# First stage's gates: own key dropped from the backward scan, sums of batch 0 by identity products on TensorE, caps behind the exponentials, new orders

## The chip, the cores and the metric

One of the cores of a Trainium2 chip runs the whole program. The metric is device time of one launch in microseconds (us). TensorE (PE) multiplies matrices out of SBUF into PSUM, VectorE (DVE), ScalarE (ACT) and GpSimd (POOL) work elementwise, SyncE (SP) issues most transfers. Each engine runs its own list of instructions in order and waits for the others through semaphores.

## The reference

It is a two-layer model on x (4 batches, 512 positions, 512 channels): a bidirectional decay gate, attention, a second gate, and a mixture of experts. The change touches the first gate alone, of which this is computed for every batch and channel, with k = v = the side input and r = x:

```
ek  = exp(min(k, 30));   ekv = ek * k;   euk = exp(min(u + k, 30))
nf, df = forward scans  a = a * decay + ekv,  b = b * decay + ek
nb, db = the same scans backward
num = nf + nb - ekv + euk * k
den = df + db - ek  + euk
c   = sigmoid(x) * num / max(den, 1e-8) * (0.8 + 0.2 * tf)
```

The value c goes, as a high and a low half (fp32r), into the query, key and value products of the attention.

## The kernel before

Channels lie on the partitions, positions along the free dimension: a gate is one chunk of 128 channels by 512 positions of one batch. `first_gates` (lines 91 to 379) is the first stage: it makes the eight gates n = 0 to 7 of batches 0 and 1 (four chunks each, `KC` = 4) and the 16 query products of batch 0. The stage is one block: `attention` (from line 672) begins when all five engines have ended their lists, with projections of the key rows, a gate of its own kind (lines 1452 to 1505) and the same weight stream. After it come routing and the experts.

The order of the work is written out by hand, one list for each engine (lines 65 to 83). A letter is a step and the number its gate or its query head. On TensorE `k` and `x` are four f32 transposes each (lines 233 and 241) into `psk` (two banks) and `psx` (three banks), `v` the vectors, and `Q` a query product (`split_products`, line 668: twelve fp32r matmuls of 512 columns) into `psq` (two banks). On ScalarE `t` takes the keys out of PSUM (271), `E` is the pair of exponentials (276, 277), `h` the high half of a query weight (265), `F` the sigmoid's denominator 1 + exp(-x) (283 to 291), `c` the high half of c (295), `e` takes a query product out (301). On VectorE `m` is the pair of minima (328, 329), `s` the four scans (344, 345), `f` the fraction (352, 355, 357), `l` the low half of c (334). On GpSimd `o` is ekv (202), `p` the own-key terms euk - ek and (euk - ek) * k (206, 208), `a` the four sums (213 to 218), `q` the low half of a query weight (193). On SP `w` loads a query weight into a ring of four, `O` stores a query product, `X` stores x transposed, `K` and `n` load what the attention needs first (lines 136 to 173).

Each gate's tensors have two halves, used in turn (`n % 2`), so gate n waits for parts of gate n - 2. A query product waits for its weight's low half and for all four low halves of c of batch 0:

```python
pe.wait_ge(u_lo, j + 1)
pe.wait_ge(lo_done, KC)
if j >= 2:
    pe.wait_ge(q_left, j - 1)
```

`dec`, the decays that the scans read, lies in PSUM; in the attention stage the decays lie in SBUF. Elsewhere in the program line 2170 adds a transposed f32 tile onto an open PSUM bank with four f32 products by the identity for each of 16 row tiles, and lines 1061 to 1063 are the fp32r products of the attention's scores, 128 to 512 columns wide.

## Time and profile before

| what | value |
|---|---|
| median of 3 runs | 2301.48 us (2299.45 to 2307.04) |
| the profiled execution | 2301.87 us, span 2300.2 us |
| TensorE busy | 2137.5 us (93%), 11247 matmul records |
| VectorE, ScalarE, GpSimd busy | 1366.6, 1160.0, 1439.5 us |
| granted clock, mean | 0.975 |

Slices of the span, in tenths of busy time (each slice is 57.5 us, so the first stage is the first two):

```profile
PE   2899999999999999999788989999999999999996
DVE  7868888778856676766854633333333333333386
ACT  4477777777767777667562123333333333333310
POOL 7887877788745656666661402456667777753355
```

TensorE is at nine tenths or more in most slices and has its lowest share, two tenths, in the first. The chain that ended last has 32% of the span on TensorE, most of it in the experts, and none of its listed lines lies in the first stage.

### The profile page before, as it was taken

Reading aid. Unit: us, or ns where it says so; the run is one execution under the profiler, and the core shown is the slowest. Engines: PE = TensorE matmul, PEld = TensorE weight load, DVE = VectorE, ACT = ScalarE, POOL = GpSimd, SP = SyncE. Lnnn points to the kernel's source line nnn. Section 1 sums busy time; section 2 is a strip of 40 time slices with the busy share of each in tenths; the row PEclk is TensorE's granted clock in tenths of the full one; section 3 lists DMA queues with packets and bytes.
Section 4 is the critical chain, followed back from the end, with each engine's and each line's share of the span. In section 5 each row is a group of like instructions: output and inputs, shape, how many; then the busy total and the mean of one; then the engine's idle time right before and its main releaser. Section 6 shows DMA issues by size and latency. Waiting matters only on the chain. (4 is left out here: it accounts for less than half of the span.)

```text
span 2300.2 us, 39953 instructions
## 1 busy us (share of the span) xinstructions
PE 2137.5 (93%) x11247; PEld 1860.9 (81%) x11247; DVE 1366.6 (59%) x2499; ACT 1160.0 (50%) x2491; POOL 1439.5 (63%) x961
## 2 busy tenths in 40 slices
PE   2899999999999999999788989999999999999996
PEld 1678888888878878777677869988999999998875
DVE  7868888778856676766854633333333333333386
ACT  4477777777767777667562123333333333333310
POOL 7887877788745656666661402456667777753355
PEclk9999999999999999999897999999999999999998
DMA  5444444543365546665345544556667666664666
GB/s 129 142 124 130 129 133 160 170 126 97 123 216 169 161 119 206 215 203 173 91 134 220 193 153 135 159 156 194 182 188 213 193 209 186 197 197 127 179 196 207
DMA packets 368185, 381.34 MB, mean 166 GB/s; under 512 B 51572, under 2 KB 283576, under 8 KB 363256
## 3 DMA queue, kind: packets, MB, share of 16 engines
q1 hardware_dynamic: 256136, 253.25, 35.9%
q10 hardware_dynamic: 96496, 75.28, 10.7%
q0 software_dynamic: 15360, 50.34, 6.7%
q8 instruction: 109, 1.79, 0.3%
q14 instruction: 84, 0.69, 0.1%
HBM read 265.26 MB, written 121.63 MB: 168 GB/s over the span
## 5 line engine op out<-in xcount | busy, mean ns | idle before, releaser
L2061 POOL TENSOR_SCALAR we_high<-we_raw 128x1408 fp32r<-128x1408 f32 (+1 forms) x94 | 132.3, 1408 | 306.1 <-PE up_e L668 230.4
L2063 POOL TENSOR_TENSOR we_low<-we_raw,we_high 128x1408 fp32r<-128x1408 f32 (+1 forms) x94 | 312.3, 3322 | 7.8
L2276 DVE TENSOR_TENSOR hidden_e<-silu_e,up_e 128x352 f32<-128x352 f32 x127 | 66.2, 521 | 248.3 <-ACT silu_e L2215 248.3
L2259 DVE TENSOR_TENSOR hT_low<-hT_ps,hT_high 128x256 fp32r<-128x256 f32 x127 | 53.9, 425 | 254.4 <-ACT hT_high L2201 254.4
L2215 ACT ACTIVATE silu_e<-gate_e 128x352 f32<-128x352 f32 x127 | 59.1, 466 | 282.0 <-PE up_e L668 270.9
L668 PE MATMUL gate_e<-we_high,xT_high 128*128 x508 | 176.2, 347 | 15.6 <-DVE xT_low L2266 10.4
L2220 ACT ACTIVATE rows_out<-down_e 128x512 f32<-128x512 f32 x127 | 76.0, 599 | 199.4 <-PE down_e L668 199.4
L668 PE MATMUL gate_e<-we_high,xT_low 128*128 x508 | 164.6, 324 | 0.0
L668 PE MATMUL gate_e<-we_low,xT_high 128*128 x508 | 164.1, 323 | 0.0
L668 PE MATMUL up_e<-we_high,xT_high 128*128 x508 | 164.0, 323 | 0.0
L668 PE MATMUL up_e<-we_high,xT_low 128*128 x508 | 163.7, 322 | 0.0
L668 PE MATMUL up_e<-we_low,xT_high 128*128 x508 | 163.1, 321 | 0.0
L668 PE MATMUL down_e<-we_high,hT_high 128*128 x381 | 150.0, 394 | 2.6 <-issue 2.6
L668 PE MATMUL down_e<-we_low,hT_high 128*128 x381 | 150.9, 396 | 0.0
L668 PE MATMUL down_e<-we_high,hT_low 128*128 x381 | 150.8, 396 | 0.0
L1438 DVE TENSOR_TENSOR pT_low<-weights_T,pT_high 128x512 fp32r<-128x512 f32 (+1 forms) x192 | 108.1, 591 | 66.4 <-ACT pT_high L1256 65.1
L942 POOL TENSOR_TENSOR q_low<-q_raw,q_high 128x512 fp32r<-128x512 f32 x64 | 104.1, 1629 | 69.0 <-ACT q_high L1222 68.9
L1239 ACT ACTIVATE prob<-scores,neg_max 128x128 f32<-128x128 f32 (+3 forms) x256 | 131.6, 530 | 17.9 <-DVE neg_max L1423 17.7
L1423 DVE CUSTOM_DVE_ANT_0 scores<-scores,mask 128x128 f32<-128x128 f32 (+3 forms) x256 | 118.0, 522 | 36.5 <-PE scores L1063 36.4
L1248 ACT ACTIVATE prob<-prob,row_inv 128x128 f32<-128x128 f32 (+3 forms) x256 | 122.8, 557 | 26.0 <-DVE row_inv L1431 26.0
L938 POOL TENSOR_TENSOR wV_low<-w_ring,wV_high 128x512 fp32r<-128x512 f32 x64 | 87.6, 1376 | 66.0 <-ACT wV_high L1204 66.0
L938 POOL TENSOR_TENSOR wO_low<-w_ring,wO_high 128x512 fp32r<-128x512 f32 x64 | 95.8, 1504 | 43.2 <-ACT wO_high L1204 43.1
(389 smaller groups left out, 7180.5 us busy)
## 6 DMA issues: line engine op xcount, KB each, us to landing
slots_out<-rows_out ACTq DMA_DIRECT2D x127, 256.0 KB, 2.5
rows_early<-slots_in ACTq DMA_DIRECT2D x500, 64.0 KB, 3.4
we_raw<-L_ffn_w_gate SPq DMA_DIRECT2D x32, 704.0 KB, 4.9
we_raw<-L_ffn_w_up SPq DMA_DIRECT2D x32, 704.0 KB, 5.2
w_ring<-L_attn_Wq SPq DMA_DIRECT2D x64, 256.0 KB, 3.3
q_T<-q_out SPq DMA_DIRECT2D x64, 256.0 KB, 2.5
w_ring<-L_attn_Wk SPq DMA_DIRECT2D x64, 256.0 KB, 3.7
w_ring<-L_attn_Wv SPq DMA_DIRECT2D x64, 256.0 KB, 3.7
```

Source lines behind the costliest of these rows:

```text
L668: last = nc.tensor.matmul(out, a, b, start=start and i == 0, stop=stop and i == len(terms) - 1)
L938: tt(w_split(*u, 1), ring[:, i % RING, :], w_split(*u, 0).bitcast(F32), ALU.subtract).then_inc(u_lo, 1)
L942: tt(head(ql, n), head_raw(n), head(qh, n).bitcast(F32), ALU.subtract).then_inc(q_lo, 1)
L1239: last = nc.scalar.activation(prob[:, n % 2, P_AT[i]:P_AT[i] + w], pss[x_][:, at:at + w], ACT.Exp, scale=-1.0, bias=nmax[:, n % 2, i:i + 1 ...
L1248: nc.scalar.activation(w, w, ACT.Copy, scale=rinv[:, n % 2, i:i + 1]).then_inc(s_norm, 1)
L1423: last = nc.vector.tensor_tensor_reduce(out=acc, in0=acc, in1=mask[:, S - w:], scale=-1.0, scalar=HUGE, op0=ALU.add, op1=ALU.min, accum_ou ...
L1438: tt(ptl[:, at:at + w], pst[(3 * n + x_) % 2][:, 0:w], pth[:, at:at + w].bitcast(F32), ALU.subtract).then_inc(t_lo, 1)
L2061: nc.gpsimd.tensor_scalar(wh[:, p, at:to], raw[:, at:to], 1.0, 1.0, ALU.mult, ALU.mult).then_inc(w_hi, 1)
L2063: nc.gpsimd.tensor_tensor(wl[:, p, at:to], raw[:, at:to], wh[:, p, at:to].bitcast(F32), ALU.subtract).then_inc(w_split, 1)
L2215: nc.scalar.activation(sg[:], psg[:], ACT.Silu).then_inc(s_done, 1)
L2220: nc.scalar.activation(yb[:, p, :], psy[p][:], ACT.Copy).then_inc(y_ev, 1)
L2276: nc.vector.tensor_tensor(hb[:], sg[:], psu[:], ALU.mult).then_inc(h_done, 1)
```

## The change

- **Caps.** ScalarE takes the exponentials straight from the key's PSUM bank, uncapped, with u as the bias of the second one. GpSimd then caps both at exp(30) (and at 3.0e38). The minima of VectorE and the step `E` are gone.
- **Backward scan.** It writes b[t] = (b[t+1] + src[t+1]) * decay over 511 columns, the last column being zero: the backward sum without the own key. The own-key terms then are euk and euk * k alone, one product on GpSimd in place of a difference and a product.
- **Sums.** For gates 0 to 3 TensorE adds eu, df, db into `psq[1]` and dk, nf, nb into `psq[0]` by products with the identity (step `a` in its list); the fraction reads both banks, and the factor and the reciprocal lie in `x_stage` (SBUF) in place of `psx`. For gates 4 to 7 GpSimd adds as before, four sums.
- **Orders.** All five lists are new. `l3` moves behind `s4`, `x5` and `k7` among the query products, and the loads `w`, `K`, `n` ahead of stores.

The diff, cut to its core:

```diff
@@ -38,6 +38,8 @@
 NEG, HUGE = -2.0 ** 100, 3.0e38
 CONSTS = 8
+EXP_30 = float(np.exp(np.float32(30.0)))
+
 V_BQ, V_BK, V_BV, V_W1, V_W2, V_U1, V_U2, V_BO, V_N = 0, 16, 32, 48, 52, 56, 60, 64, 68
@@ -63,24 +65,21 @@
 FIRST_PE = (
-    "k0 v0 k1 x0 k2 x1 k3 k4 x2 k5 k6 x3 x4 k7 x5 Q0 Q1 Q2 Q3 Q4 x6 Q5 Q6 Q7 Q8 Q9 Q10 x7 Q11 Q12 Q13 Q14 Q15 "
+    "k0 v0 k1 x0 k2 x1 a0 k3 x2 a1 k4 a2 x3 k5 a3 x4 k6 Q0 Q1 Q2 x5 Q3 Q4 k7 Q5 Q6 x6 Q7 Q8 Q9 Q10 x7 Q11 Q12 Q13 Q14 Q15 "
 ).split()
 FIRST_ACT = (
-    "t0 t1 E0 E1 h0 F0 t2 h1 E2 h2 h3 t3 c0 F1 h4 E3 t4 h5 c1 h6 F2 h7 F3 E4 F4 t5 h8 E5 c2 h9 c3 e0 t6 h10 e1 t7 "
-    "h11 E6 e2 F5 e3 e4 F6 e5 c4 E7 e6 e7 h12 e8 h13 e9 c5 h14 e10 e11 h15 F7 e12 c6 e13 e14 c7 e15 "
+    "t0 t1 h0 F0 h1 t2 F1 h2 h3 c0 t3 F2 h4 h5 h6 c1 t4 h7 h8 F3 h9 c2 t5 h10 h11 h12 c3 F4 e0 t6 h13 h14 e1 h15 e2 c4 "
+    "F5 e3 e4 t7 c5 e5 e6 F6 e7 e8 e9 c6 e10 F7 e11 e12 e13 c7 e14 e15 "
 ).split()
 FIRST_DVE = (
-    "m0 m1 s0 s1 m2 f0 m3 l0 s2 f1 m4 l1 s3 f2 m5 f3 l2 l3 s4 m6 s5 f4 m7 s6 f5 l4 s7 f6 l5 f7 l6 l7 "
+    "s0 s1 f0 s2 l0 f1 s3 l1 f2 l2 f3 s4 l3 s5 f4 l4 s6 f5 l5 s7 f6 l6 f7 l7 "
 ).split()
 FIRST_POOL = (
-    "o0 p0 o1 p1 a0 a1 o2 q0 p2 q1 q2 o3 q3 a2 p3 q4 q5 a3 o4 q6 p4 q7 q8 o5 q9 p5 q10 a4 q11 o6 a5 p6 o7 p7 q12 "
-    "q13 a6 q14 a7 q15 "
+    "o0 p0 o1 p1 q0 q1 o2 p2 q2 q3 q4 o3 p3 q5 q6 q7 o4 p4 q8 q9 q10 o5 p5 q11 a4 q12 o6 p6 q13 a5 q14 q15 o7 p7 a6 a7 "
 ).split()
 FIRST_SP = (
-    "w4 w5 w6 w7 w8 w9 w10 O0 w11 O1 O2 w12 O3 X4 X5 w13 O4 w14 O5 O6 O7 O8 w15 O9 X6 O10 O11 K0 n0 O12 X7 n1 O13 "
-    "n2 O14 O15 n3 "
+    "w4 w5 w6 w7 w8 w9 w10 w11 w12 w13 w14 w15 O0 X4 O1 O2 O3 X5 O4 O5 O6 O7 K0 n0 O8 n1 O9 X6 O10 n2 O11 n3 O12 X7 O13 O14 O15 "
 ).split()
-
 def turns(order, **steps):
@@ -186,7 +185,7 @@
             pool.wait_ge(ident_steps, 2)
             nc.gpsimd.memset(zero[:], 0.0).then_inc(ident_steps, 1)
             pool.wait_ge(ident_steps, 3)
-            tt = nc.gpsimd.tensor_tensor
+            tt, ts = nc.gpsimd.tensor_tensor, nc.gpsimd.tensor_scalar
             def low(j):
                 pool.wait_ge(u_hi, j + 1)
@@ -196,28 +195,31 @@
             def first_product(n):
                 p = n % 2
                 pool.wait_ge(exp_done, n + 1)
+                ts(ek[:, p, :], ek[:, p, :], EXP_30, HUGE, ALU.min, ALU.min).then_inc(min_done, 1)
+                ts(eu[:, p, :], eu[:, p, :], EXP_30, HUGE, ALU.min, ALU.min).then_inc(min_done, 1)
                 if n >= 2:
                     pool.wait_ge(scan_done, n - 1)
-                    pool.wait_ge(sums_done, 2 * (n - 1))
+                pool.wait_ge(min_done, 2 * n + 1)
                 tt(ekv[:, p, :], ek[:, p, :], kt[:, p, :], ALU.mult).then_inc(products_done, 1)
-            def other_products(n):
+            def other_product(n):
                 p = n % 2
-                tt(dl[:, p, :], eu[:, p, :], ek[:, p, :], ALU.subtract).then_inc(products_done, 1)
-                pool.wait_ge(products_done, 3 * n + 2)
-                tt(dk[:, p, :], dl[:, p, :], kt[:, p, :], ALU.mult).then_inc(products_done, 1)
+                if 2 <= n < KC + 2:
+                    pool.wait_ge(added, n - 1)
+                pool.wait_ge(min_done, 2 * n + 2)
+                tt(dk[:, p, :], eu[:, p, :], kt[:, p, :], ALU.mult).then_inc(products_done, 1)
             def sums(n):
                 p = n % 2
                 pool.wait_ge(scan_done, n + 1)
-                tt(nb[:, p, :], nf[:, p, :], nb[:, p, :], ALU.add)
-                tt(db[:, p, :], df[:, p, :], db[:, p, :], ALU.add).then_inc(sums_done, 1)
-                pool.wait_ge(sums_done, 2 * n + 1)
-                pool.wait_ge(products_done, 3 * n + 3)
-                tt(nf[:, p, :], nb[:, p, :], dk[:, p, :], ALU.add)
-                tt(df[:, p, :], db[:, p, :], dl[:, p, :], ALU.add).then_inc(sums_done, 1)
-
-            turns(FIRST_POOL, o=first_product, p=other_products, q=low, a=sums)
+                tt(df[:, p, :], df[:, p, :], db[:, p, :], ALU.add)
+                tt(nf[:, p, :], nf[:, p, :], nb[:, p, :], ALU.add).then_inc(sums_done, 1)
+                pool.wait_ge(sums_done, 2 * (n - KC) + 1)
+                pool.wait_ge(products_done, 2 * n + 2)
+                tt(df[:, p, :], df[:, p, :], eu[:, p, :], ALU.add)
+                tt(nf[:, p, :], nf[:, p, :], dk[:, p, :], ALU.add).then_inc(sums_done, 1)
+
+            turns(FIRST_POOL, o=first_product, p=other_product, q=low, a=sums)
         @block.tensor
         def _(pe):
@@ -228,7 +230,7 @@
                 if n >= KC:
                     pe.wait_ge(k_in[0], 16 + 16 * KC)
                 if n >= 2:
-                    pe.wait_ge(kt_done, n - 1)
+                    pe.wait_ge(exp_done, n - 1)
                 for t in range(TC):
                     last = nc.tensor.transpose(psk[n % 2][:, t * P:(t + 1) * P], kin[:, n, t, :], ident[:])
                 last.then_inc(k_T, 1)
@@ -249,11 +251,22 @@
                 split_products(nc, psq[j % 2][:], [((qwh[:, j, k, :], qwl[:, j, k, :]), (ch[:, 0, k, :], cl[:, 0, k, :]))
                                                    for k in range(KC)], True, True).then_inc(q_mm, 1)
+            def add(n):
+                p = n % 2
+                pe.wait_ge(scan_done, n + 1)
+                pe.wait_ge(products_done, 2 * n + 2)
+                if n:
+                    pe.wait_ge(c_steps, 3 * n)
+                for ps_, parts in ((psq[1], (eu, df, db)), (psq[0], (dk, nf, nb))):
+                    for i, part in enumerate(parts):
+                        last = nc.tensor.matmul(ps_[:], ident[:], part[:, p, :], start=i == 0, stop=i == 2)
+                last.then_inc(added, 1)
+
             def vectors(n):
                 pe.wait_ge(v_in, 16 * (len(vec) + 1))
                 nc.tensor.transpose(psv, rows[:], ident[0:V_N, 0:V_N]).then_inc(x_T, 1)
-            turns(FIRST_PE, k=keys, v=vectors, x=rows_x, Q=queries)
+            turns(FIRST_PE, k=keys, v=vectors, x=rows_x, a=add, Q=queries)
         @block.scalar
         def _(act):
@@ -265,16 +278,18 @@
                 nc.scalar.activation(qwh[:, j, :, :].rearrange("p k m -> p (k m)"), qraw[:, j % QR, :], ACT.Copy).then_inc(u_hi, 1)
             def keys(n):
+                p, i = n % 2, n % KC
                 act.wait_ge(k_T, n + 1)
                 if n >= 2:
-                    act.wait_ge(products_done, 3 * (n - 1))
-                nc.scalar.activation(kt[:, n % 2, :], psk[n % 2][:], ACT.Copy).then_inc(kt_done, 1)
-
-            def exponentials(n):
-                p = n % 2
-                act.wait_ge(min_done, n + 1)
-                nc.scalar.activation(ek[:, p, :], ek[:, p, :], ACT.Exp)
-                nc.scalar.activation(eu[:, p, :], eu[:, p, :], ACT.Exp).then_inc(exp_done, 1)
+                    act.wait_ge(products_done, 2 * (n - 1))
+                    act.wait_ge(scan_done, n - 1)
+                    if n < KC + 2:
+                        act.wait_ge(added, n - 1)
+                    else:
+                        act.wait_ge(sums_done, 2 * (n - KC - 1))
+                nc.scalar.activation(ek[:, p, :], psk[p][:], ACT.Exp)
+                nc.scalar.activation(kt[:, p, :], psk[p][:], ACT.Copy)
+                nc.scalar.activation(eu[:, p, :], psk[p][:], ACT.Exp, bias=cols[:, V_U1 + i:V_U1 + i + 1]).then_inc(exp_done, 1)
             def factor(n):
                 i, px = n % KC, psx[n % XR]
@@ -284,11 +299,15 @@
                 else:
                     if n >= KC + 2:
                         act.wait_ge(xt_out, 16 * (n - KC - 1))
+                    else:
+                        act.wait_ge(c_steps, 3 * (n - 1))
                     nc.scalar.activation(xst[:, n % 2, :], px[:], ACT.Identity,
                                          bias=cols[:, V_BO + i:V_BO + i + 1]).then_inc(x_left, 1)
                 nc.scalar.activation(px[:], px[:], ACT.Exp, scale=-1.0).then_inc(factor_steps, 1)
                 act.wait_ge(factor_steps, 2 * n + 1)
-                nc.scalar.activation(px[:], px[:], ACT.Identity, bias=one[:]).then_inc(factor_steps, 1)
+                if 2 <= n < KC:
+                    act.wait_ge(c_steps, 3 * (n - 1))
+                nc.scalar.activation(xst[:, n % 2, :] if n < KC else px[:], px[:], ACT.Identity, bias=one[:]).then_inc(factor_steps, 1)
             def c_high(n):
                 act.wait_ge(c_steps, 3 * n + 3)
@@ -310,24 +329,16 @@
             turns(order[:1], t=keys)
             act.wait_ge(t_chain, 1)
             nc.scalar.activation(small[:, 20:24], small[:, 16:20], ACT.Exp, scale=-1.0).then_inc(s_chain, 1)
-            turns(order[1:], t=keys, E=exponentials, h=high, F=factor, c=c_high, e=queries)
+            turns(order[1:], t=keys, h=high, F=factor, c=c_high, e=queries)
         @block.vector
         def _(dve):
             nc.vector.memset(one[:], 1.0)
+            for last_of in (nb, db):
+                nc.vector.memset(last_of[:, :, S - 1:S], 0.0)
             dve.wait_ge(v_in, 16 * (len(vec) + 1))
             nc.vector.tensor_reduce(small[:, 16:20], te[:], AX.X, ALU.add).then_inc(t_chain, 1)
             dve.wait_ge(cols_done, 1)
-
-            def minima(n):
-                p, i = n % 2, n % KC
-                dve.wait_ge(kt_done, n + 1)
-                if n >= 2:
-                    dve.wait_ge(products_done, 3 * (n - 1))
-                    dve.wait_ge(scan_done, n - 1)
-                nc.vector.tensor_scalar(ek[:, p, :], kt[:, p, :], 30.0, None, ALU.min)
-                nc.vector.tensor_scalar(eu[:, p, :], kt[:, p, :], cols[:, V_U1 + i:V_U1 + i + 1], 30.0, ALU.add,
-                                        ALU.min).then_inc(min_done, 1)
             def low(n):
                 dve.wait_ge(hi_done, n + 1)
@@ -336,28 +347,36 @@
             def scans(n):
                 p = n % 2
-                dve.wait_ge(products_done, 3 * n + 1)
+                dve.wait_ge(products_done, 2 * n + 1)
                 if n >= 2:
                     dve.wait_ge(c_steps, 3 * (n - 1))
+                    if n < KC + 2:
+                        dve.wait_ge(added, n - 1)
                 col = dec[:, n:n + 1].broadcast_to([P, S])
-                for f, b, src in ((nf, nb, ekv), (df, db, ek)):
+                after = dec[:, n:n + 1].broadcast_to([P, S - 1])
+                for f, b, src in ((df, db, ek), (nf, nb, ekv)):
                     nc.vector.tensor_tensor_scan(f[:, p, :], col, src[:, p, :], 0.0, ALU.mult, ALU.add)
-                    last = nc.vector.tensor_tensor_scan(b[:, p, ::-1], col, src[:, p, ::-1], 0.0, ALU.mult, ALU.add)
+                    last = nc.vector.tensor_tensor_scan(b[:, p, 0:S - 1][:, ::-1], src[:, p, 1:S][:, ::-1], after, 0.0,
+                                                        ALU.add, ALU.mult)
                 last.then_inc(scan_done, 1)
             def fraction(n):
                 p, px = n % 2, psx[n % XR]
-                dve.wait_ge(sums_done, 2 * n + 2)
+                if n < KC:
+                    dve.wait_ge(added, n + 1)
+                    num, den, fac = psq[0][:], psq[1][:], xst[:, p, :]
+                else:
+                    dve.wait_ge(sums_done, 2 * (n - KC) + 2)
+                    num, den, fac = nf[:, p, :], df[:, p, :], px[:]
                 dve.wait_ge(factor_steps, 2 * n + 2)
-                nc.vector.scalar_tensor_tensor(out=df[:, p, :], in0=df[:, p, :], scalar=1e-8, in1=px[:],
+                nc.vector.scalar_tensor_tensor(out=df[:, p, :], in0=den, scalar=1e-8, in1=fac,
                                                op0=ALU.max, op1=ALU.mult).then_inc(c_steps, 1)
                 dve.wait_ge(c_steps, 3 * n + 1)
-                nc.vector.reciprocal(px[:], df[:, p, :]).then_inc(c_steps, 1)
+                nc.vector.reciprocal(fac, df[:, p, :]).then_inc(c_steps, 1)
                 dve.wait_ge(c_steps, 3 * n + 2)
-                nc.vector.scalar_tensor_tensor(out=px[:], in0=nf[:, p, :], scalar=par1[:, n // KC, n % KC, 2:3], in1=px[:],
+                nc.vector.scalar_tensor_tensor(out=px[:], in0=num, scalar=par1[:, n // KC, n % KC, 2:3], in1=fac,
                                                op0=ALU.mult, op1=ALU.mult).then_inc(c_steps, 1)
-            minima(0)
             dve.wait_ge(s_chain, 3)
             nc.vector.tensor_scalar(small[:, 24:28], small[:, 20:24], 1.0, None, ALU.add).then_inc(t_chain, 1)
             dve.wait_ge(t_chain, 2)
```

## Rows read from the trace of the kernel before

**Rows 1.** Windows of 20 us: length, busy time (instructions) of PE, PEld, DVE, ACT, POOL, clock, DMA.

```profile
20.00:40.00 20.00, 3.23 (x13) 2.52 (x14) 19.90 (x19) 8.02 (x15) 19.69 (x17) 1.00 0.23 63
...
80.00:100.00 20.00, 20.00 (x91) 16.28 (x90) 18.86 (x17) 10.07 (x18) 19.69 (x16) 1.00 0.55 168
```

**Rows 2.** Timeline of VectorE, 16 to 64: start, duration, instruction, idle before.

```profile
16.31 1.21 DVE L344 TENSOR_TENSOR_SCAN g_nf<-vec_ps,g_ekv 128x512 f32<-128x512 f32 x1
...
25.24 0.39 DVE L328 TENSOR_SCALAR g_ek<-g_kt 128x512 f32<-128x512 f32 x1
...
26.96 0.67 DVE L352 SCALAR_TENSOR_TENSOR g_df<-g_df,psx 128x512 f32<-128x512 f32 x1
...
31.73 0.52 DVE L328 TENSOR_SCALAR g_ek<-g_kt 128x512 f32<-128x512 f32 x1
...
62.73 1.45 DVE L334 TENSOR_TENSOR c_low<-psx,c_high 128x512 fp32r<-128x512 f32 x2
```

**Rows 3.** Timeline of all engines at the first stage's end and the attention's start.

```profile
109.84 0.39 PE L668 MATMUL psq<-c_high,wq_low 128*128 128x512 f32 x1
...
111.07 0.68 ACT L301 ACTIVATE q_out<-psq,bqs 128x512 f32<-128x512 f32 x1
112.18 0.50 SPq L160 DMA_DIRECT2D w_ring<-L_attn_Wv  x1
...
113.19 0.42 PEld L1114 LDWEIGHTS proj<-ident,k_rows 128*128 128x128 f32 x4 [3.38 <-issue]
...
116.08 0.63 ACT L1204 ACTIVATE wV_high<-w_ring 128x512 fp32r<-128x512 f32 x1 [0.72 <-DMA w_ring<-L_attn_Wv]
```

**Rows 4.** Timeline of TensorE: first query product, and a start behind a gap in attention.

```profile
64.33 0.77 PE L668 MATMUL psq<-c_high,wq_high 128*128 128x512 f32 x1
64.89 0.63 PE L668 MATMUL psq<-c_low,wq_high 128*128 128x512 f32 x1
65.32 0.63 PE L668 MATMUL psq<-c_high,wq_low 128*128 128x512 f32 x1
...
66.48 0.39 PE L668 MATMUL psq<-c_high,wq_low 128*128 128x512 f32 x1
...
962.17 1.09 PE L1114 MATMUL proj<-ident,k_rows 128*128 128x128 f32 x4 [5.01 <-DVE v_low L1401]
...
963.17 0.41 PE L1062 MATMUL scores<-k_low,q_high 128*128 128x128 f32 x1
963.38 0.41 PE L1063 MATMUL scores<-k_high,q_low 128*128 128x128 f32 x1
```

**Rows 5.** GpSimd: a timeline row, then groups by form (busy us, mean ns | idle).

```profile
13.43 1.26 POOL L202 TENSOR_TENSOR g_ekv<-g_ek,g_kt 128x512 f32<-128x512 f32 x1 [11.28 <-ACT g_eu L277]
...
L2061 POOL TENSOR_SCALAR we_high<-we_raw 128x1408 fp32r<-128x1408 f32 x62 | 85.1, 1372 | 230.4 <-PE up_e L668 230.4
...
L2085 POOL TENSOR_SCALAR we_high<-we_raw 64x512 fp32r<-64x512 f32 x1 | 0.6, 615 | 0.0
```

**Rows 6.** VectorE's groups by form: dearest scan, and a reciprocal in SBUF.

```profile
L1458 DVE TENSOR_TENSOR_SCAN g_db<-par,g_ek 128x512 f32<-128x512 f32 x24 | 49.0, 2040 | 0.0
...
L1500 DVE RECIPROCAL g_db<-g_df 128x256 f32<-128x256 f32 x16 | 27.9, 1743 | 0.0
```

**Rows 7.** f32 on TensorE: loads of four transposes, then line 2170 between others.

```profile
14.52 0.87 PEld L241 LDWEIGHTS psx<-ident,xin 128*128 128x128 f32 x4
...
2201.18 1.05 PE L2170 MATMUL xT_ps<-ident,xT 128*128 128x128 f32 x8
2201.99 0.48 PE L668 MATMUL xT_ps<-we_high,expert_rows_more 128*128 128x512 f32 x1
```

**Rows 8.** Windows around two starts behind gaps, columns as in rows 1.

```profile
114.00:120.00 6.00, 4.77 (x11) 3.80 (x12) 2.30 (x3) 3.34 (x7) 5.92 (x12) 0.51 0.90 272
...
962.00:967.00 5.00, 4.83 (x17) 4.48 (x18) 3.52 (x11) 3.65 (x5) 0.00 (x0) 0.50 0.79 281
```

**Rows 9.** Timeline of ScalarE: the first keys leave PSUM.

```profile
10.59 0.58 ACT L271 ACTIVATE g_kt<-psk 128x512 f32<-128x512 f32 x1
```

4 lines of the change are left out of this document (2 added, 2 removed).

## The prediction

> **What bounds the kernel now.** I read the page's table of slices first: the diff touches only lines 66 to 379, and the stretch that these lines fill is the first 113 us of 2300. Then the windows of 20 us: in the four from 20 to 100 (the first and the last stand in the rows) VectorE is busy 18 to 20 of 20 us and GpSimd 19.7, while TensorE has 3 us of work at 20:40 and is full at 80:100 [rows 1]. So it has two halves. In the first, gates of batch 0 are made by VectorE and GpSimd and TensorE waits; in the second, TensorE makes 16 query products without a gap. The hinge is the fourth low half of c (line 334, `l3`): `Q0` waits for `lo_done >= 4`. It ends at 62.73 + 1.45 = 64.18 [rows 2], the first product starts at 64.33 and the last matmul starts at 109.84 [rows 3]; the attention stage starts at 113.19 [rows 3]. What comes behind follows from there with nothing that is tied to absolute time, so the kernel's change is the shift of 113.19 and little else. From 64.33 on, the products are back to back: 192 matmuls, from the sixth (66.48) to the last (109.84) 0.228 us each if the two groups of transposes among them take 0.43 [rows 3, 4], so relief of GpSimd or VectorE behind that point is worth nothing; what counts is when `l3` comes.
>
> **Prices.** Eight scans go from 16.31 to 25.24, 1.116 us each [rows 2]; a gate has four (4.46). A fraction (lines 352, 355, 357) goes from 26.96 to 31.73, 4.77 us [rows 2]. A pair of minima takes 25.24 to 26.96, 1.72 [rows 2]. A GpSimd tensor_tensor takes 1.26 [rows 5].
>
> **Parts that take work away.** The minima leave VectorE: five pairs stand before `l3` (m1 to m5), some 8.6 us. The reciprocal writes to SBUF instead of PSUM: from SBUF to SBUF 256 columns take 1.74 [rows 6], so 512 3.5, next to the same within the 4.77, no change. The backward scan has one column less and its two operations exchanged; bounds 1.1 (as now) to 2.0 (the dearest scan row of the trace [rows 6]); I take 1.116, as the decay operand stays in PSUM as in the rows of this stage. At the upper end the ten backward scans before `l3` would cost 9 us; I keep that for the range's upper part. On GpSimd a gate of batch 0 falls from 7 tensor_tensor to 2 plus two caps. A cap is a tensor_scalar: 64 partitions by 512 takes 0.615, 128 by 1408 takes 1.37 [rows 5]; 0.5 to 0.75, taken 0.6. GpSimd then has idle time in the whole first half, so its errors cost nothing. ScalarE gets three reads of each key bank in place of one plus two from SBUF: the same count.
>
> **The part that adds: the sums on TensorE.** For gates 0 to 3 six products with the identity, 512 columns of f32, stand between scans and fraction; call their time A. They begin after `scan_done` and, as both PSUM banks are single, after the fraction before (`c_steps >= 3n`). The fraction waits for `added`. So fraction and sums of batch 0 run in one chain, (A + 4.8) per gate, where before GpSimd's four sums (some 5.1 us) ran beside VectorE's work for another gate.
>
> The only f32 product by the identity in the trace is line 2170. Its 4 calls are 8 records, from 2201.18 to 2201.99 [rows 7], so two records a call, 0.10 us a record of 128 columns at the full clock. The f32 transposes at half clock take 0.87 for four, 0.21 each [rows 7]. Neither tells the price of 512 columns: at half clock an fp32r matmul of 128 columns takes 0.21 too [rows 4], while 512 columns take 0.43, so at 128 columns something other than the columns sets the pace. Lower end: twelve records at the fp32r pace, 12 x 0.228 = 2.7 us at 2.4 GHz and 12 x 0.43 = 5.1 at 1.2. Upper end: the record scaled by its columns, 12 x 4 x 0.21 = 10.2 at 1.2 GHz and half of that, 5.1, at 2.4 (by the 0.10, 4.9). I take the upper price: both operands are f32, a call needs two loads of the identity, and if the moving operand is handled in parts like the stationary one each load must meet both parts. The Trainium skill, FP8 and Floating Point Precision, section TensorE Precision Notes, says true FP32 is four passes; by it A would be 5.1 to 10.2, by the lower pace 2.7 to 5.1, and no row here decides.
>
> The clock: behind the last product TensorE has a gap with four transposes at 113.19 in it [rows 3], and the granted clock of 114:120 is 0.51, which is 1.2 GHz [rows 8]. At 962 the same: 0.50 for 5 us of matmuls [rows 8] behind a gap of 5.01 [rows 4]. At 64.33 the slow pace lasted until near 66.48 [rows 4]. Between two sums lie 4.8 us of fraction, with one or two groups of transposes: a gap like these. So each A starts or soon falls to 1.2 GHz and stays there for t = 2.1 to 5.3 us or more: A = 5.1 + t/2, 6.2 to 7.8 (8.5 at t = 6.8). Taken 7.5. The Trainium skill (TensorE: Matmul & The Clock Gate, section What's actually happening) puts it as a throttled default that activity releases. It speaks against placing short bursts on an idle TensorE, and the rows of 114:120 agree.
>
> **The walk to `l3`.** Keys 0 leave PSUM from 10.59 [rows 9]; three ACTIVATEs of 0.55 to 12.3, two caps 13.5, product 14.8; scans of gate 0 to 19.3. Sums 0 to 26.8, fraction 0 to 31.6; before it ended at 31.73, so until here nothing is lost. Sums 1 to 39.1, fraction 1 to 43.9. A new wait: ScalarE takes keys 3 only when sums 1 are done, as they read `eu` of that half. Keys 3 out at 40.8, then `F2` and `h4`, then on GpSimd `q4` stands ahead of the caps and product; scans of gate 3 start at about 47.2, not 44, so scans and `l1` end at 52.3, 0.9 behind sums 2 (51.4). Fraction 2 to 57.1. Sums 3 to 64.6, fraction 3 to 69.4 (before 62.73 [rows 2]). The new order then has `s4` ahead of `l3`: 4.46, and 0.6 for `l3`: 74.4. Against 64.18 that is +10.2. VectorE waits some 16 us for `added` and `products_done` on this way, more than the 8.6 that the minima gave back.
>
> **From `l3` to the end.** The products' 45.5 us (64.33 to 109.84) stay. Among them stand four groups of transposes, not two: +0.8 (0.43 each, half of the 0.87). Product 7 waits for `e5`, which stands behind `t7` and `c5` on ScalarE: +0.3; a longer slow stretch at `Q0`: +0.4. The tail gets shorter: now 109.84 to 113.19, as `e15` waits behind `c7` until 111.07 and the load `n3` is issued at 112.18 [rows 3]; after, `c7` and `n3` come earlier, so matmul, `e15` 0.69, one issue and the 0.5 of the block's end: -1.3. In attention ScalarE's wait of 0.72 at 116.08 for a weight [rows 3] can go: -0.4. GpSimd's sums of gates 4 to 7 end by 107, VectorE's last gate by 119, before the last product (121.5). Of SP's queue, the loads move ahead of the stores; stores wait only for `q_left`. Together -0.2.
>
> **Sum:** +10.2 - 0.2 = +10.0 on the profiled execution's 2301.87 (span 2300.2), 2311.9; the runs' median is 2301.48, 0.4 lower, so 2311.5.
>
> **Rivals.**
> 1. Cheap records, not slower. One pass a record and the clock up: A = 2.7. Then the sums hide under the scans, and VectorE's own work sets `l3`: five gates' scans 22.3, four fractions 19.1, four low halves 2.6 and some 3 of waits from 14.8 give 61.6, -2.6, in all -2.8: 2298.7. At A = 5.1 (the same at half clock) `l3` is at 67.2: 2304.3. Turning point A = 3.4. For it: the 128-column rows allow it; against: the two records a call.
> 2. The upper price with the clock up throughout, as products may hold it up across the fractions: A = 5.1 to 5.6, `l3` at 67.2 to 69, +3 to +4.6, 2305. Against: the slow stretches of rows 8 behind such gaps; for: those gaps have no f32 products around them, so no row shows what these do to the clock.
> 3. Bursts too short to raise the clock at all: A = 10.2, `l3` at 43.8 + 4 x 10.2 + 0.3 = 84.9, +20.5: 2322.
> 4. The relief of VectorE and GpSimd decides, over 0.3% faster: would need `l3` before 57.4, less than VectorE's own instructions allow (58.8), so only a gain in later stages could do it.
>
> **Numbers.** Forecast (A 6.2 to 8.5, +6 to +14) 0.62; rival 1 0.15; rival 2 0.12; rival 3 (and dear scans) 0.08; rival 4 0.03. 0.3% is 6.9 us, about what a measurement of this kernel tells from no change; it is reached at A = 6.4. Slower by more: 0.58 of the forecast and rival 3, 0.66. Within: 0.04 + 0.15 + 0.12 = 0.31. Faster: 0.03. Range: 2302 leaves out the cheap end of rival 1, 2320 most of rival 3.
>
> **What would show it.** In the profile after: six f32 products of two records each before every fraction of batch 0, 5.1 to 10.2 us per gate, with 1.2 GHz in part of them; VectorE idle some 3.3 (`f0`), 3 (`f1`), 3 (`s3`) and 6 us (`f3`) until `added` or `products_done`; fraction 3 ending near 69, `Q0` starting near 74.5, attention near 123. If a record of 512 columns takes 0.23 us at full clock, the price is wrong; if `Q0` starts before 68, the forecast is. If the stage's end moves by 10 but the time doesn't, the claim that nothing later is tied to absolute time is wrong.

## The result, and the profile after

The changed kernel takes 2327.3 us (median of 5 runs, 2321.2 to 2331.2), the kernel before beside it 2299.9 (2296.7 to 2307.0): ratio 1.0107, 95% interval 1.0091 to 1.0122, slower by 21 to 28 us. The forecast was 2311.5, with a range of 2302 to 2320: the sign came, and TensorE's sums took what was said, but the loss is more than twice the 10 us forecast.

The profiled execution took 2331.24 us (span 2329.5). VectorE's timeline after shows where: start, duration, instruction, idle before and its releaser [rows 2 have the same view].

```profile
17.80 1.22 DVE L358 TENSOR_TENSOR_SCAN g_df<-vec_ps,g_ek 128x512 f32<-128x512 f32 x1 [3.18 <-POOL g_ekv L203]
...
52.87 1.22 DVE L358 TENSOR_TENSOR_SCAN g_df<-vec_ps,g_ek 128x512 f32<-128x512 f32 x1 [5.89 <-POOL g_ekv L203]
...
70.06 0.69 DVE L372 SCALAR_TENSOR_TENSOR g_df<-psq,x_stage 128x512 f32<-128x512 f32 x1 [5.92 <-PE psq L262]
...
79.31 0.66 DVE L345 TENSOR_TENSOR c_low<-psx,c_high 128x512 fp32r<-128x512 f32 x1
...
101.70 0.69 DVE L372 SCALAR_TENSOR_TENSOR g_df<-g_df,psx 128x512 f32<-128x512 f32 x1 [3.06 <-POOL g_nf L220]
...
130.29 0.69 DVE L345 TENSOR_TENSOR c_low<-psx,c_high 128x512 fp32r<-128x512 f32 x1 [1.60 <-ACT c_high L314]
```

Scans of gate 0 start at 17.80 (forecast 14.8), of gate 3 at 52.87 (47.2), fraction 3 at 70.06; `l3` ends at 79.97, where it was 64.18 [rows 2] and 74.4 in the forecast. The idle times name GpSimd's `g_ekv` and, once, the identity products. GpSimd's groups in the first 136 us (busy us, mean ns | idle):

```profile
L198 POOL TENSOR_SCALAR g_ek<-g_ek 128x512 f32<-128x512 f32 x8 | 15.4, 1920 | 14.5 <-ACT g_eu L292 14.1
L199 POOL TENSOR_SCALAR g_eu<-g_eu 128x512 f32<-128x512 f32 x8 | 15.3, 1914 | 0.6
...
L203 POOL TENSOR_TENSOR g_ekv<-g_ek,g_kt 128x512 f32<-128x512 f32 x8 | 10.1, 1268 | 0.6
```

A cap takes 1.92 us, not 0.6. TensorE's timeline at the last sums and at the products:

```profile
62.94 2.04 PE L262 MATMUL psq<-g_eu,ident 128*128 128x512 f32 x2 [6.78 <-DVE psx L377]
64.77 1.82 PE L262 MATMUL psq<-g_df,ident 128*128 128x512 f32 x2
66.43 1.02 PE L262 MATMUL psq<-g_db,ident 128*128 128x512 f32 x2
67.28 1.02 PE L262 MATMUL psq<-g_dk,ident 128*128 128x512 f32 x2
...
80.11 0.77 PE L687 MATMUL psq<-c_high,wq_high 128*128 128x512 f32 x1 [9.22 <-DVE c_low L345]
...
107.93 0.77 PE L687 MATMUL psq<-c_high,wq_high 128*128 128x512 f32 x1 [5.40 <-DVE c_low L345]
...
134.10 0.39 PE L687 MATMUL psq<-c_high,wq_low 128*128 128x512 f32 x1
```

Each product by the identity is one call and shows as two records (x2). From one call to the next it is 1.7 to 1.8 us at first and 0.86 later. The same stretch in windows (columns as in [rows 1]) shows the two levels of the granted clock, 0.50 (1.2 GHz) and then near 1 (2.4 GHz):

```profile
62.00:66.00 4.00, 3.06 (x4) 1.51 (x5) 1.45 (x2) 0.60 (x1) 3.92 (x4) 0.50 0.00 0
66.00:70.00 4.00, 4.00 (x11) 1.61 (x10) 0.00 (x0) 0.00 (x0) 1.93 (x2) 0.95 0.41 115
```

The sums of gates 0 to 3 take 6.7, 7.6, 8.0 and 6.9 us (A, forecast 7.5). But the query products behind `l3` take 54.0 us (80.11 to 134.10) where they took 45.5 [rows 3, 4]: they are no longer back to back. The end of the stage, all engines [rows 3]:

```profile
134.53 0.69 ACT L320 ACTIVATE q_out<-psq,bqs 128x512 f32<-128x512 f32 x1 [2.03 <-PE psq L687]
135.24 0.36 SPq L172 DMA_DIRECT2D q_T<-q_out  x1
...
136.11 0.42 PEld L1133 LDWEIGHTS proj<-ident,k_rows 128*128 128x128 f32 x4 [2.05 <-issue]
```

Attention starts at 136.11, 22.9 later than in [rows 3].

### The profile page after: what moved, and what is told of

It is laid out like the page before. It is cut to its first block and busy times, and to the rows that moved or that the text cites. A ratio compares the mean times of both kernels' runs of the same rounds, so it can differ in the third digit from the quotient of the medians.

```text
span 2329.5 us, 40035 instructions
## 1 busy us (share of the span) xinstructions
PE 2171.9 (93%) x11295; PEld 1876.1 (81%) x11295; DVE 1361.6 (58%) x2485; ACT 1159.9 (50%) x2491; POOL 1440.6 (62%) x953
## 5 line engine op out<-in xcount | busy, mean ns | idle before, releaser
L1258 ACT ACTIVATE prob<-scores,neg_max 128x128 f32<-128x128 f32 (+3 forms) x256 | 131.4, 530 | 17.3 <-DVE neg_max L1442 17.1
```

What stands on the lines that cost most here:

```text
L1258: last = nc.scalar.activation(prob[:, n % 2, P_AT[i]:P_AT[i] + w], pss[x_][:, at:at + w], ACT.Exp, scale=-1.0, bias=nmax[:, n % 2, i:i + 1 ...
```

## The experiments

The milestones of all kernels, from their VectorE and TensorE timelines (`s0`: first scan starts; `l3`: fourth low half ends; "att.": attention's first transposes on TensorE; "rest": span minus att.), and the medians of the runs, with before on the same chip:

```
kernel                            s0     l3     att.    rest    median   before   95% of the ratio
before                          16.31  64.18  113.22  2187.0
changed                         17.80  79.97  136.14  2193.4  2327.29  2299.86  1.0091 1.0122
e1_no_caps                      20.23  80.99  130.36  2187.2  2321.68  2303.63  1.0052 1.0104
e2_products_for_minima          17.34  78.25  129.03  2188.0  2318.88  2303.63  1.0036 1.0081
e3_one_minimum                  16.98  79.72  132.86  2185.6  2321.60  2303.63  1.0052 1.0103
e4_low3_first                   17.77  77.07  136.97  2187.6  2326.36  2303.63  1.0079 1.0125
e5_no_caps_setup_first          13.54  74.00  123.42  2197.3  2323.96  2310.34  1.0030 1.0077
e6_gpsimd_sums_no_caps          14.08  67.05  117.52  2193.0  2313.65  2310.34  0.9991 1.0030
e7_four_products                17.57  75.60  132.80  2194.7  2332.55  2310.34  1.0053 1.0125
e8_scalar_caps_new_order        15.87  59.98  108.01  2194.3  2305.21  2310.34  0.9954 0.9997
e9_before_without_own_key       16.05  67.49  121.83  2181.9  2306.49  2301.27  1.0014 1.0040
e10_scalar_caps_changed_orders  15.47  76.27  126.55  2187.1  2319.10  2301.27  1.0066 1.0102
e11_early_products              14.06  55.40  101.29  2175.4  2284.66  2301.27  0.9909 0.9949
e12_outputs_ahead               17.94  81.63  139.46  2193.0  2333.83  2312.19  1.0078 1.0122
e13_cheap_caps_setup_first      15.23  74.08  124.24  2193.6  2315.85  2303.16  1.0037 1.0078
e14_changed_again               17.55  82.18  138.48  2186.9  2325.73  2303.16  1.0064 1.0112
e15_new_order_whole_products    13.97  54.54  102.54  2181.1  2287.07  2303.16  0.9912 0.9958
```

The start of attention is the finer scale (the kernel before itself took 2300 to 2312 on different chips); it still moves by 2.3 us between two profiles of one kernel (changed, e14), and every other kernel was profiled once. Shifts of 3 us (e3, e7, e12) are barely clear of that.

**e1 to e3: the caps.** e1 drops both:

```diff
-                ts(ek[:, p, :], ek[:, p, :], EXP_30, HUGE, ALU.min, ALU.min).then_inc(min_done, 1)
-                ts(eu[:, p, :], eu[:, p, :], EXP_30, HUGE, ALU.min, ALU.min).then_inc(min_done, 1)
```

> The changed kernel without its two caps on GpSimd (leaves out the minimum with 30, which is computed nowhere in stage 1). T1 (the caps, 1.92 us each, stand on the chain and cost what the forecast lacked): scans of gate 0 start at 14.0 instead of 17.8, fraction 3 ends near 67.5 instead of 74.8, Q0 near 76, attention's first instruction at 136.1 - 12 = 124, time 11 to 12 below the changed kernel (2315). Rival R1 (the forecast's: their size does not matter, 1.2 us per gate hidden except once): -3 at s0, -3 at s3, none later, attention near 130, time 2321. Rival R2 (the surplus comes from the orders and the clock, not the caps): attention stays within 3 of 136.

Attention came at 130.4, 5.8 earlier, and the time at 2321.7: the numbers of R1, 6 us short of T1. But R1's steps did not come. It had gate 0 start 3 us earlier, and gate 0 starts 2.4 later than with the caps, at 20.2, for a reason in none of the theories. VectorE's timeline of e1:

```profile
13.86 0.18 DVE L379 RECIPROCAL small<-small 128x4 f32<-128x4 f32 x1
14.07 0.99 DVE L381 TENSOR_SCALAR small<-small 128x4 f32<-128x4 f32 x1
...
15.16 1.13 DVE L385 TENSOR_TENSOR par<-small 128x16 f32<-128x16 f32 x1
16.21 0.17 DVE L388 COPY par<-cols 128x16 f32<-128x16 f32 x1
16.29 1.24 DVE L389 COPY par<-small 128x16 f32<-128x16 f32 x1
...
18.76 1.24 DVE L390 TENSOR_SCALAR bqs<-cols 128x16 f32<-128x16 f32 x1
20.03 0.17 DVE L392 COPY vec_ps<-par 128x8 f32<-128x8 f32 x1
```

and GpSimd's beside it:

```profile
13.75 1.28 POOL L206 TENSOR_TENSOR g_dk<-g_eu,g_kt 128x512 f32<-128x512 f32 x1
14.98 1.27 POOL L200 TENSOR_TENSOR g_ekv<-g_ek,g_kt 128x512 f32<-128x512 f32 x1
16.22 1.28 POOL L206 TENSOR_TENSOR g_dk<-g_eu,g_kt 128x512 f32<-128x512 f32 x1
```

Sixteen elements take 1.1 to 1.2 us, and each long instruction ends within 0.1 us of the end of a GpSimd product; every second one passes in between, 0.17 us. In e1 the set-up runs beside GpSimd's products; the kernel before did it while GpSimd was idle.

e2 exchanges only the operation, e3 drops only the second minimum:

```diff
-                ts(ek[:, p, :], ek[:, p, :], EXP_30, HUGE, ALU.min, ALU.min).then_inc(min_done, 1)
+                ts(ek[:, p, :], ek[:, p, :], 1.0, 1.0, ALU.mult, ALU.mult).then_inc(min_done, 1)    # e2
+                ts(ek[:, p, :], ek[:, p, :], EXP_30, None, ALU.min).then_inc(min_done, 1)           # e3
```

> Each cap (two minima by constants) becomes two multiplications by 1.0, of the same shape and the same tile in place (leaves out the minimum with 30). T1a (it is the operation that is dear on GpSimd: 1.92 us of minimum against 0.50 to 0.97 of product, as the 1408-column instruction at 0.97 ns a column suggests): these instructions take 0.5 to 0.7 us, attention starts near 126, time 9 to 10 below the changed kernel. Rival T1b (the slot is dear: in place, beside ScalarE's writes or the VectorE scans): they stay at 1.9 us and nothing moves.

> The second, idle minimum (by the largest float) is taken out of each cap; the cap itself stays. If GpSimd is paid per minimum: 1.92 us falls to 1.0 to 1.3, attention near 129 (-7), time 7 below the changed kernel. If a minimum costs one fixed slow pass, whatever stands second: 1.9 stays and nothing moves.

A row of e2's and one of e3's GpSimd timeline:

```profile
15.87 0.62 POOL L198 TENSOR_SCALAR g_ek<-g_ek 128x512 f32<-128x512 f32 x1
```

```profile
18.19 1.49 POOL L198 TENSOR_SCALAR g_ek<-g_ek 128x512 f32<-128x512 f32 x1
```

Two multiplications 0.62, one minimum 1.49, two minima 1.91: T1a holds, the slot is innocent. Each reading of e3 was half wrong: the first minimum costs 0.9 more than two multiplications, the second 0.4. Attention moved by 7.1 and 3.3, both less than said (10 and 7). In e2 the held set-up is a reason: it ends at 17.3, and gate 0 starts behind it without another wait. In e3 it ends at 15.3 and gate 0 waits 1.71 more for `g_ekv`, so there it is only the cap that fell by 0.4 instead of 0.6 to 0.9.

**e5: the held set-up.** e1 with one instruction moved:

```diff
-            turns(order[:1], t=keys)
             act.wait_ge(t_chain, 1)
             nc.scalar.activation(small[:, 20:24], small[:, 16:20], ACT.Exp, scale=-1.0).then_inc(s_chain, 1)
+            turns(order[:1], t=keys)
```

> The changed kernel without caps, as in e1 (leaves out the minimum with 30), and besides ScalarE computes the small exponential (128x4, 0.21 us) that VectorE's twelve small set-up instructions wait for ahead of gate 0's three keys activations instead of behind them. In e1 these twelve ran from 12.57 to 20.2 instead of in 2.0 us: each second one of them took 1.0 to 1.25 us and ended when a GpSimd product ended. T4 (VectorE's small copies and tensor_scalars are held while a GpSimd tensor_tensor runs, and this gave back 6 of the 12 us that the caps' removal frees): with the set-up over by 12.7, before GpSimd's first product, each takes 0.17, scans of gate 0 start near 14, attention near 124 to 125 instead of 130.36, time near 2316. Rival R4 (the set-up was slow by itself, or removal of the caps frees only 6 us anyway since later waits take over): s0 starts earlier, but attention stays within 2 of 130.

Each small instruction takes 0.16 to 0.18 now. Gate 0 starts at 13.54, 6.7 earlier, and attention at 123.4, 6.9 earlier, so T4 holds and R4 falls. The time (2324.0, +13.6 on before) is above the 2316 named, on a chip where before took 2310.3, not 2303.6. Against before, e5 loses 13.6, e1 18.0 and the changed kernel 22.6 to 27.4; the intervals of e1 and e5 (12 to 24, 7 to 18) overlap.

**e13: the forecast's own price.**

```diff
+                ts(ek[:, p, :], ek[:, p, :], 1.0, 1.0, ALU.mult, ALU.mult).then_inc(min_done, 1)    # and the set-up as in e5
```

> The changed kernel at the forecast's own price for a cap: each cap is two multiplications by 1.0 (0.62 us in e2; leaves out the minimum with 30), and the set-up runs ahead of gate 0 as in e5. All else as changed. If the cap's price and the held set-up are all that the forecast's walk to l3 lacked, scans of gate 0 start at 14.8, l3 ends at 74 to 76 (forecast 74.4). Attention: 123.2 by the forecast's flat 48.8 us from l3; T8 (the second half is not flat: the products wait for gates 4 to 7 by 2 to 4 us even so) says 125.5 to 127.5.

`l3` ends at 74.08 (forecast 74.4), attention starts at 124.24 (forecast 123.2, T8 at least 125.5): given its price for a cap the forecast's walk was right, to `l3` and behind it; T8 falls. The products' longest wait there is 0.98. The kernel takes 12.7 us more than before (8 to 18), where 10.0 was forecast. That the milestones agree within 1 us is partly luck, as one kernel moves by 2. e13 moves the set-up too, but that is not what its gain comes from: in the changed kernel the set-up ends at 14.62, and gate 0 waits 3.18 us longer for `g_ekv`.

**e4 and e12: orders.** e4: `f3 l3 s4` on VectorE for `f3 s4 l3`. e12: `e3 e4 e5 e6 t7 c5 F6` on ScalarE for `e3 e4 t7 c5 e5 e6 F6`.

> Only VectorE's order: l3 ahead of s4 instead of behind it. In both theories Q0 starts 4 us earlier, near 76. T1 (the second half is set by the chain of gates 4 to 7 over GpSimd's caps, which starts with s4 at 75.5 and holds e5 back, so that the products wait anyway): the 5.4 us wait of the products before Q7 grows to near 9, attention's start stays within 1 of 136, time unchanged. Rival R3 (as the forecast has it: from l3 to the end the products' 54 us are unbroken work behind l3): attention near 132, time -4.

> The changed kernel with ScalarE's e5 and e6 ahead of t7 and c5 instead of behind them: the products' one long wait (5.40 us before Q7, in the changed kernel) was for e5, which stood behind t7 and c5. T7 (that wait is a symptom: the chain of gates 4 to 7, scans, sums, cap and fraction, ends the stage with l7 at 131, and any wait of the products taken away here comes back before x7 or a later product): the wait before Q7 goes, others come in its place, attention between 135.5 and 138 (136.1 without the edit, the few tenths to 1.3 by which t7 and gate 7 come later), time same. Rival R7 (the order in ScalarE's queue cost the 5.4 us, as the forecast's +0.3 for the same item assumed in kind): attention near 131, time -5.

In e4 `Q0` starts at 77.22, 2.9 earlier (4 expected), and attention 0.8 later. TensorE's waits there:

```profile
77.22 0.77 PE L687 MATMUL psq<-c_high,wq_high 128*128 128x512 f32 x1 [5.54 <-DVE c_low L345]
...
91.26 0.77 PE L687 MATMUL psq<-c_high,wq_high 128*128 128x512 f32 x1 [3.44 <-ACT q_out L320]
...
108.74 0.77 PE L687 MATMUL psq<-c_high,wq_high 128*128 128x512 f32 x1 [3.83 <-DVE c_low L345]
```

Two waits of 3.4 and 3.8 for one of 5.4 (one near 9 was expected). In e12 the 5.4 become 1.70 and 3.71; attention is at 139.5, above the range given (`l3` is 1.7 later there too), and nothing is won. R3 and R7 fall. With the caps as they are the products' waits are a symptom: gates 4 to 7 follow one another in a ring, in which each gate waits for the buffers of the gate two before it (scans, sums, keys, caps, product, scans), and ScalarE's queue hands their lateness on to the products, at `e5` or at a later one. In the changed kernel ScalarE takes keys 7 when the sums of gate 5 are done, then come the caps, the product and the scans:

```profile
101.78 0.60 ACT L290 ACTIVATE g_ek<-psk 128x512 f32<-128x512 f32 x1 [4.88 <-POOL g_nf L220]
...
104.21 1.91 POOL L198 TENSOR_SCALAR g_ek<-g_ek 128x512 f32<-128x512 f32 x1
106.20 1.91 POOL L199 TENSOR_SCALAR g_eu<-g_eu 128x512 f32<-128x512 f32 x1
108.19 1.28 POOL L203 TENSOR_TENSOR g_ekv<-g_ek,g_kt 128x512 f32<-128x512 f32 x1
...
109.51 1.22 DVE L358 TENSOR_TENSOR_SCAN g_df<-vec_ps,g_ek 128x512 f32<-128x512 f32 x1 [1.58 <-POOL g_ekv L203]
```

Even without any such wait, `l7` ends at 131.0, and the soonest that a stage ended behind it was 2.2 us (e11): an order that leaves `l7` where it is could win 3 us at most. An order that was not tried is GpSimd's: `g_ekv` needs the first cap alone but stands behind both, 1.9 us in every gate.

**e6, e7: the identity products.** e6 is e5 with the four GpSimd tensor_tensors for all gates (`added` gone, `a0` to `a3` in GpSimd's order). e7 is the changed kernel with

```diff
-                for ps_, parts in ((psq[1], (eu, df, db)), (psq[0], (dk, nf, nb))):
+                for ps_, parts in ((psq[1], (eu, df)), (psq[0], (dk, nf))):
```

> As e5_no_caps_setup_first (leaves out the minimum with 30), but the sums of gates 0 to 3 are GpSimd's four tensor_tensors again, as gates 4 to 7 have them, and no identity products. T2 (the identity products, 6.7 to 8.0 us a gate on the chain fraction, products, fraction, set gates 1 to 3): fraction 3 ends near 58 instead of 67.5, Q0 near 67, attention 9 earlier than in e5_no_caps_setup_first, near 115, time -9. Rival R2 (GpSimd becomes the bound in their place, 16 instructions of 1.22 more): less than 3.

> The changed kernel with four identity products per gate instead of six in gates 0 to 3 (leaves out the backward sum there), caps as they are. T2: each group 7.3 -> 4.9; gates 1 to 3 each gain up to 2.4, fraction 3 ends 5 to 6 earlier (near 69), attention near 130.5, time -5 to -6. If the caps' chain alone bounded the stage, under 2.

e6: `l3` 7.0 earlier, attention 5.9 (9 expected; gate 2 waits 3.59 for GpSimd, whose order was not written for this). e7: `l3` 4.4, attention 3.3 (5 to 6 expected). Its groups took 5.2 to 6.1 us, not 4.9, as more of a shorter group runs at the lower clock, and the ring behind `l3` takes the rest. R2 falls, and T2 holds in kind: without caps the products cost some 6 us over GpSimd's sums. In the times e6 shows it (+3.3 on before, where e5 has +13.6); e7's +22.2 does not differ from the changed kernel's.

**e9: the own key alone**, on the kernel before:

```diff
-                tt(dl[:, p, :], eu[:, p, :], ek[:, p, :], ALU.subtract).then_inc(products_done, 1)
-                tt(dk[:, p, :], dl[:, p, :], kt[:, p, :], ALU.mult).then_inc(products_done, 1)
+                tt(dk[:, p, :], eu[:, p, :], kt[:, p, :], ALU.mult).then_inc(products_done, 1)
+                    dve.wait_ge(sums_done, 2 * (n - 1))    # in the minima: eu is read by the sums now
```

> The kernel before with one part of the change: the backward scan without the own key, so that GpSimd's subtraction (1.26 us a gate, 10 us in the stage) goes and the sums add g_eu itself. Its orders, minima and GpSimd sums stay. T5 (lifetime: g_eu is now read by the last sums, so VectorE's minima of gate n+2, which overwrite it, must wait for the sums of gate n, where they waited for the subtraction; the freed GpSimd time is smaller than that wait): the gates come 2 to 8 us later, attention at 115 to 121 against 113.2, time 2 to 7 above the kernel before. Rival R5 (relief: GpSimd is among the busiest engines of the stage, so 10 us less of it bring 2 to 5 us): attention at 108 to 111.

+5.2 us, interval 3.2 to 9.2, attention 8.6 later (a little above T5's range): eight instructions fewer on a busy engine make it slower. VectorE's timeline of e9, at the minima of gate 2:

```profile
25.93 1.30 DVE L329 TENSOR_SCALAR g_ek<-g_kt 128x512 f32<-128x512 f32 x1 [0.90 <-POOL g_df L216]
27.15 1.48 DVE L330 TENSOR_SCALAR g_eu<-g_kt,cols 128x512 f32<-128x512 f32 x1
```

They wait for the last sum; before they started at 25.24 without one [rows 2]. The first one also takes 1.30 beside a GpSimd sum, where it took 0.39, so fraction 0 starts 1.6 later. R5 falls. How much of the 8.6 is this buffer's life was not tried apart (a third buffer would).

**e10, e8, e11, e15: the cap on ScalarE**, nothing left out:

```diff
+                nc.scalar.activation(ek[:, p, :], psk[p][:], ACT.Relu, bias=room[:, KC:KC + 1], scale=-1.0)
+                nc.scalar.activation(eu[:, p, :], psk[p][:], ACT.Relu, bias=room[:, i:i + 1], scale=-1.0).then_inc(capped, 1)
                 nc.scalar.activation(kt[:, p, :], psk[p][:], ACT.Copy)
+                act.wait_ge(capped, n + 2)
+                nc.scalar.activation(ek[:, p, :], ek[:, p, :], ACT.Exp, bias=room[:, KC:KC + 1], scale=-1.0)
+                nc.scalar.activation(eu[:, p, :], eu[:, p, :], ACT.Exp, bias=room[:, KC:KC + 1], scale=-1.0).then_inc(exp_done, 1)
```

(`room` holds 30 - u and 30.) e8 has besides GpSimd's sums for all gates and new orders, on VectorE `s0 s1 f0 s2 f1 l0 s3 f2 l1 f3 l2 l3 s4 s5 f4 f5 ...`; e11 and e15 also

```diff
-                    num, den, fac = nf[:, p, :], df[:, p, :], xst[:, p, :] if n < KC else px[:]
+                    num, den, fac = nf[:, p, :], df[:, p, :], px[:]
+            def early(j):    # e11 alone: k 0 to 2 of products 0 and 1 ahead of l3
+                pe.wait_ge(lo_done, KC - 1)
+                some_products(j, 0, KC - 1)
```

> The changed kernel, all of its computation, identity products and orders kept, but the cap on ScalarE (two Relu activations more per gate, 1.2 us) in place of GpSimd's two minima (3.84 us), and the set-up ahead of gate 0. T1 and T4 (the place of the cap cost 12, the products the rest): gate 0 scans at 15.5 to 16, fraction 3 ends at 68 to 71, attention at 125 to 127, which is 9 to 11 below the changed kernel's 136.1, and still 12 above before; time 2312 to 2316 where before takes 2301 to 2304. If ScalarE's 1.2 us a gate are as dear as GpSimd's 3.84, since they stand on the same chain, attention at 130 or later.

> All of the computation kept. The cap on ScalarE: exp(30 - relu(30 - k)) and exp(30 - relu(30 - u - k)), two Relu activations more per gate (0.6 each), none on GpSimd; sums of all gates on GpSimd, without the own-key subtraction; set-up ahead of gate 0; five orders written anew so that gates 0 to 3 follow each other on VectorE (9.8 us a gate: four scans 4.46, fraction 4.77, low half 0.6). T1, T2 and T4 together: fraction 3 near 54 to 56, Q0 near 57 to 60, attention's first instruction at 105 to 109 against 113.2 of the kernel before, time 4 to 8 below the kernel before. Rival: GpSimd (78 us of tensor_tensor in 96) or ScalarE (1.2 us a gate more) slips, and attention comes at 113 or later.

> All of the computation kept. As e8_scalar_caps_new_order, with four more edits: the factor of gates 0 to 3 is back in its PSUM bank (in e8 the two scalar_tensor_tensors of a fraction with all operands in SBUF took up to 1.75 us beside GpSimd, against 0.69 with one in PSUM); each exponential signals by itself, so that GpSimd's product of ek starts 1.2 us earlier; the first two query products do three of their four accumulation steps before the last low half; orders anew. T6: the products run without a gap from their start to the end of the stage (e8: 60.1 to 106), so 18 of 24 matmuls of 0.23 us that start before `l3` bring 3 to 4 us, and the chain to l3 another 2 to 4: fraction 3 near 54 to 56, attention at 101.5 to 104.5 (e8: 108.0, before: 113.2), time 9 to 12 below the kernel before. Rival R6: the stage's end passes to the chain of gates 4 to 7 on VectorE and GpSimd (its l7 ends at 103.2 in e8), so that the products stall later and attention stays within 1.5 of 108.

> All of the computation kept. e11_early_products without the early three steps of the first two products (its orders written anew for that; the factor in PSUM and the separate signals stay). If the split brought 3 to 4 of the 6.7 us between e8 (108.0) and e11 (101.3): attention at 104 to 105.5. If the chain to l3 brought it all: 101 to 102.5.

e10: 126.6, as said (the time, +17.8 on before, is 3 us above what was named). e8: 108.0 and -5.1 us (interval 1 to 11 faster), as said, though `l3` at 59.98 was later than meant. A reason is in VectorE's timeline of e8 (gates 3 and 4):

```profile
52.69 1.75 DVE L367 SCALAR_TENSOR_TENSOR g_df<-g_df,x_stage 128x512 f32<-128x512 f32 x1 [0.56 <-POOL g_nf L217]
...
69.87 0.69 DVE L367 SCALAR_TENSOR_TENSOR g_df<-g_df,psx 128x512 f32<-128x512 f32 x1 [0.98 <-POOL g_nf L217]
```

The same line with both inputs in SBUF takes up to 1.75 beside GpSimd, with one in PSUM 0.69. e15 puts it back into PSUM, lets GpSimd start after the first exponential and has new orders (the three were not tried apart): `l3` 54.54, attention 102.5, -16.1 us. e11 adds the early products, with orders of its own. Its last matmuls and the end of VectorE's list:

```profile
96.89 0.39 PE L688 MATMUL psq<-c_high,wq_low 128*128 128x512 f32 x1
...
97.66 1.45 DVE L352 TENSOR_TENSOR c_low<-psx,c_high 128x512 fp32r<-128x512 f32 x2
```

The products end near 97, 3.6 earlier than in e15, but attention comes at 101.3, 2.2 us behind `l7` (101.5 to 104.5 was expected). So the split brought 1.2 us, not 3 to 4: R6's number (within 1.5 of 108) is wrong, but its kind, that gates 4 to 7 end the stage, took the rest. e11 is the fastest: 2284.7 against 2301.3, ratio 0.9929 (0.9909 to 0.9949), 12 to 21 us faster than before, and by the two ratios some 37 to 41 faster than the changed kernel.

**e14: the changed kernel again.** No edit.

> The changed kernel once more, nothing edited, for what its first profile left open: there the attention started 22.9 later, but the span was 29.3 longer, as from the attention's start to the end it took 2193.4 us and in the profile before 2187.0. T9 (the rest does not depend on the change and scatters with the chip and the run by some 6): here the attention starts at 135.5 to 137.5 again, the rest takes what the other kernels of this call take within 4, and the time against before on the same chip is +22 to +26. Rival R9 (a later stage is slowed by what the first leaves behind): the rest takes 6 more than in the two other kernels of the call, whichever chip it is.

Attention starts at 138.48, 1.0 above the range given; the time, +22.6 (15 to 26), is inside it. The rest is 2186.9, as in the kernel before (2187.0), with 2193.6 (e13) and 2181.1 (e15) beside it on the same chip. "Within 4 of the others" fails, but so does R9: the rest scatters from 2175 to 2197 over all kernels, and the 6.4 us of the first profile are of that kind.

## Why the prediction was wrong

- **That only the first stage counts**: right within the scatter of the rest (e14). **The hinge, that the coming of `l3` decides**: right at cheap caps (e13), wrong with the caps as they are, where `l3` 2.9 earlier brought nothing (e4).
- **A, the sums on TensorE**: right in price and clock, 6.7 to 8.0 for 7.5; one product costs 0.86 us at 2.4 GHz and 1.7 to 1.8 at 1.2, against 0.228 for one matmul of a query product. The Trainium skill, FP8 and Floating Point Precision, section TensorE Precision Notes, gives true FP32 four passes; the trace agrees, at 0.86 / 0.228 = 3.8.
- **Scans and fraction**: right (1.11 from scan to scan, reciprocal 3.35, fraction 4.78).
- **The failed step: "0.5 to 0.75, taken 0.6. GpSimd then has idle time in the whole first half, so its errors cost nothing."** Size and cover were both wrong. The rows that I priced from are two multiplications by 1.0 (lines 2061 and 2085); a cap of two minima takes 1.92. And an engine that is idle between gates covers nothing that stands inside a gate: a key bank is read only when the sums of two gates earlier are done, and then caps, product and scans follow one another (s3: 5.89 us idle for `g_ekv`). e13 against the changed kernel: 5.9 us at `l3`, 11.9 at attention. The ends of the range came from A and from dear scans and allowed nothing for a dearer cap, so the range missed. Rival 3 (2322) lies nearest to 2327, but it is not what happened: its A was 10.2.
- **"The products' 45.5 us stay"**: right at cheap caps (74.23 to 122.20, 48.0 with the two more groups of transposes and slow start, of 47.0 said), wrong at dear ones: 54.0. GpSimd's work of gates 4 to 7 was said to end by 107 and VectorE's last gate by 119; they end at 107.4 and 119.1 in e13, and at 121 and 131 in the changed kernel. That the product stall would be 0.3 us for `e5` was the visible part of this; it was 5.4, and moving `e5` does not help (e12).
- **`s4` ahead of `l3`, +4.46**: right for `Q0`, but worth nothing at the end of this kernel (e4), since the ring of gates 4 to 7 sets it.
- **Tail -1.3**: right (last matmul to attention 2.0, was 3.35). Attention's -0.4 did not show: the wait of 0.72 is gone, but ScalarE's next one for a weight is as long as before (3.75, was 3.83).
- **Overlooked**: VectorE's set-up passed from an idle GpSimd's time to a busy one's. In the changed kernel the minima let most of it through, but e2, which differs from e13 only by it, starts gate 0 2.1 us and attention 4.8 us later (the four groups of identity products took 2 us more in e2, which is of the scatter named above, so 4.8 may be too much).

The sum, by profiles: 10.0 forecast + 1.0 (e13's 124.24 against 123.2) + 11.9 for the caps' price = 22.9 (14.2 and 25.3 by e14's profile). The medians, +27.4 and +22.6, agree with that within their intervals. The same price shows with nothing left out: e10, with the cap on ScalarE and the set-up first, starts attention 9.6 earlier.
